# A soft mixture of slots, taken two batches at a time, in a four-layer early-fusion network

## Chip, cores and metric

The kernel runs on one core of a Trainium2 chip as a single program. Its time is the device time of that core in microseconds; the kernel before takes 2536.07 us (median of three runs, 2534.09 to 2538.44). Engine names: PE is TensorE, DVE VectorE, ACT ScalarE, POOL GpSimd, SP SyncE, which issues most DMAs.

## The reference

Sixteen batches, each of 64 image tokens (patches times a matrix) and 128 text tokens, so 192 tokens of width 192. Then four layers, each an attention and a feed-forward part on layer-normalised rows, both added to `h`:

- layer 0: softmax attention, then 8 gated experts, two for each token; layer 1: quantised attention, then 16 experts with GELU, two for each token;
- layer 2: attention with random features, then a tree of 21 nodes; layer 3: softmax attention with 12 heads, then the soft mixture of slots.

The mixture, for x = layernorm(h), 64 experts with 16 slots each (1024 slots):

```
phi_n  = phi * rsqrt(sum over experts of phi^2 + 1e-6)
logits = x . phi_n                       # (batch, 192 tokens, 1024 slots)
D = softmax of logits over the tokens;  C = softmax of logits over the slots
Xs = D^T x                               # 1024 slots of 192 columns
Ys = w2(gelu(w1(layernorm(Xs)) + b1)) + b2   # by expert; hidden width 384
h  = h + C Ys
```

All is float32.

## The kernel before

**Tiles.** `h` lies on 96 partitions: a batch is two tiles of 96 rows by 192 columns, 32 tiles in all, also in the slot stage. `k.xnT` and `phi` have their 192 columns as two halves of 96 rows.

**experts()** (line 480) serves the expert stages of layers 0 and 1. Each of 64 and 56 tiles takes 128 rows. On POOL's queue `fetch(n)` (issue at L539) gathers the rows of tile n into one of three buffers as soon as tile n-3 is turned, and `give(n)` (L545) scatters the answers of tile n when the last product's copy is out. The loop over n issues fetch(n+3), then give(n). PE turns the rows (L564), multiplies them into the hidden columns over 128 rows (L572) and over the other 64 (L578: matmuls of 64 rows, upper and lower half of the array in turn), and down (L584).

**attention3()** (L1543) works in steps of one batch. In a step PE, DVE and ACT take half of the heads at a time, `u`: PE writes logits, DVE takes their lowest (L1860), ACT the exp of the turned ones (L1799), and so on; POOL gives the root of the row variances (L1623), DVE normalises the rows of a coming batch (L1841, L1846). The finished batch is stored to `kept` in device memory and its sums over the rows are taken by take_stats. After the loop `norm_stats` (L150) makes shift and scale of all rows in one block, with a table load on ACT (L186).

**slots_ffn()** (L2372) goes by four quarters of 256 slots (16 experts). `prepare` normalises all rows of `h` on ACT (L2781), turns them, and finds for each token the lowest and highest of its logits over all 1024 slots with rough (bf16) products on PE (L2613) and reduces on DVE (L2874); the result, `low_of`, goes to device memory and comes back by batch as `tok`, spread over 128 partitions, in a ring of three. Then a pass over the 16 batches makes the slots of quarter 0 (`first`), then the quarter's experts run, and in passes 1 to 3 (`both`) the slots of one quarter are made while the answers of the quarter before are weighed and added; `last` weighs those of quarter 3 and writes the output.

In a pass one batch b goes through:
1. PE `make_logits`: 8 matmuls, 96 rows deep, into bank b % 2.
2. DVE `lowest` (L2879) and `shifted` (L2887), which adds `tok` and leaves the combine logits in a ring of HELD = B + 8 batches.
3. ACT `exp_disp` (L2803) with its sum; `exp_combine` (L2808).
4. PE `turn_disp` (bank 4), ACT `keep_disp` (L2820).
5. PE `make_slots` (L2660): 8 matmuls into bank 2 + b % 2.
6. DVE `spread` (sums L2895, aggregates L2901), POOL the root (L2568), DVE `norm` (L2914, L2916).
7. PE `turn_slots` (bank 5), ACT `keep_rows` (L2812).
8. In `both`, LAG = 5 batches behind: PE `weigh` (L2683, 8 matmuls that write 96 rows, bank 6 + b % 2), DVE `add` (L2925). Its answers `ys` come from `s_y` in device memory in FETCHED = 4 buffers.

SP issues, batch by batch and in that order, the tokens (L2469) and the answers (L2476). Every engine's order is written out by hand in its own steps(); nothing plans it. The slot experts' matmuls are L2736 (128 rows), L2742 (64 rows, halves) and L2756.

## Time and profile before

| | |
|---|---|
| median of three runs | 2536.07 us |
| profiled execution, its own time | 2539.78 us |
| its span, from first to last instruction | 2538.0 us |
| mean granted clock of TensorE | 0.956 of full |
| busy: PE, DVE, ACT, POOL | 91%, 52%, 34%, 20% |
| matmuls (L2660, make_slots) | 512, 99.4 us busy, 338 ns each |
| matmuls (L2683, weigh) | 512, 97.3 us busy |
| tokens and answers from memory, share of the last chain | s_tok 2% |

"Busy" counts the time in which an engine executes; matmuls are pipelined and overlap, so that PE's busy share tells only that it hardly stood idle. The mean of one matmul counts its latency and is longer than the distance between two in a stream. The last chain is followed back from the last instruction. Idle time is put down to what ended it.

### The profile page before, as it was taken

The page shows a single profiled execution, that of the slowest core. Times are in us where ns is not written, and L with a number is a line of the kernel's source. Part 1 is how long each engine was busy: PE and PEld are TensorE (multiplying, and loading weights), DVE is VectorE, ACT ScalarE, POOL GpSimd, SP SyncE. Part 2 cuts the span into 40 slices and gives each one's busy share as a digit, 9 for nine tenths or more (in the row PEclk, how much of TensorE's full clock was granted, in tenths as well). Part 3 has the DMA queues.
Part 4 walks back from the last instruction along what each step waited for, and adds up shares of the span by engine and source line. Part 5 has one row for each costly group of instructions (what it writes and reads, how often), then busy time and mean ns, then how long its engine had stood idle before and what let it go on. Part 6 is the DMA issues. An engine that isn't in the chain of part 4 may idle for free. (4 is left out here: it accounts for less than half of the span.)

```text
span 2538.0 us, 52883 instructions
## 1 busy us (share of the span) xinstructions
PE 2315.0 (91%) x18339; PEld 2043.3 (81%) x18339; DVE 1318.6 (52%) x3939; ACT 870.4 (34%) x2148; POOL 514.7 (20%) x621
## 2 busy tenths in 40 slices
PE   9968999997993899998999899999788999999997
PEld 9957999996882789897888787777557888888886
DVE  2664333335996311113888746655576274462744
ACT  2411222223882233332333324433344242432430
POOL 1223233222341444442222100000121010010100
PEclk9979999998995899999999899999899999999999
DMA  4124555521111777672000000000002724527265
GB/s 117 30 53 133 157 149 172 159 77 43 48 30 35 198 235 205 204 216 62 20 20 6 1 14 8 7 7 7 15 16 74 196 71 120 151 57 200 73 159 158
DMA packets 234546, 235.04 MB, mean 93 GB/s; under 512 B 29736, under 2 KB 214942, under 8 KB 234270
## 3 DMA queue, kind: packets, MB, share of 16 engines
q1 hardware_dynamic: 220638, 203.56, 29.0%
q0 software_dynamic: 11520, 27.54, 3.4%
q10 hardware_dynamic: 2240, 1.99, 0.3%
q8 instruction: 90, 1.47, 0.2%
q14 instruction: 58, 0.48, 0.1%
HBM read 277.77 MB, written 35.45 MB: 123 GB/s over the span
## 5 line engine op out<-in xcount | busy, mean ns | idle before, releaser
L572 PE MATMUL f_pg<-f_vxT,f_w 128*128 128x128 f32 x2112 | 260.7, 278 | 3.1 <-DVE f_vxT L642 3.1
L572 PEld LDWEIGHTS f_pg<-f_vxT,f_w 128*128 128x128 f32 x2112 | 256.1, 195 | 4.6 <-DVE f_vxT L642 4.6
L584 PE MATMUL f_po<-f_wd,f_hid 128*128 128x192 f32 x1440 | 254.3, 326 | 1.2 <-DVE f_vout L668 0.6
L584 PEld LDWEIGHTS f_po<-f_wd,f_hid 128*128 128x128 f32 x1440 | 231.2, 190 | 2.0 <-issue 1.7
L545 POOL DMA_INDIRECT f_answers<-f_vout,f_to_row x120 | 118.8, 990 | 423.0 <-DVE f_vout L666 250.4
L653 DVE TENSOR_TENSOR f_hid<-f_silu,f_pg 128x128 f32<-128x128 f32 x336 | 81.8, 284 | 207.1 <-ACT f_silu L621 191.9
L621 ACT ACTIVATE f_silu<-f_pg 128x128 f32<-128x128 f32 x336 | 78.5, 277 | 292.6 <-PE f_pg L578 272.8
L626 ACT ACTIVATE f_hid<-f_pg,f_b 128x128 f32<-128x128 f32 x384 | 106.3, 376 | 196.8 <-PE f_pg L578 196.8
L578 PE MATMUL f_pg<-f_vxT,f_wr 64*128 64x128 f32 x2112 | 151.2, 285 | 0.0
L2568 POOL TENSOR_TENSOR s_small<-s_small,s_half 128x2 f32<-128x2 f32 x64 | 44.5, 695 | 511.3 <-DVE s_small L2904 511.3
L2974 DVE TENSOR_TENSOR s_y<-s_bank,s_b 128x384 f32<-128x384 f32 x64 | 35.5, 558 | 205.2 <-PE s_bank L2756 172.7
L2756 PE MATMUL s_bank<-s_w,s_arena 128*128 128x192 f32 x768 | 135.0, 333 | 7.6 <-DMA s_b<-s_b_of 7.6
L2756 PEld LDWEIGHTS s_bank<-s_w,s_arena 128*128 128x128 f32 x768 | 125.6, 192 | 18.0 <-issue 9.3
L578 PEld LDWEIGHTS f_pg<-f_vxT,f_wr 64*128 64x128 f32 x2112 | 128.1, 188 | 14.7 <-issue 0.6
L642 DVE COPY f_vxT<-f_pt 128x256 f32<-128x256 f32 x120 | 50.6, 422 | 161.2 <-PE f_pt L564 161.2
L2851 ACT ACTIVATE s_arena<-s_bank,s_b 128x256 f32<-128x256 f32 x192 | 73.6, 482 | 165.8 <-PE s_bank L2742 165.8
L539 POOL DMA_INDIRECT f_vrows<-f_normed,f_from_row x120 | 117.0, 975 | 43.2 <-issue 35.6
L2660 PE MATMUL s_bank<-h,s_arena 96*128 96x192 f32 x512 | 99.4, 338 | 21.9 <-ACT s_arena L2820 21.2
L2683 PE MATMUL s_bank<-s_ys,s_combine 128*96 128x193 f32 x512 | 97.3, 339 | 15.7 <-DMA s_ys<-s_y 9.7
L2803 ACT ACTIVATE s_arena<-s_bank,s_small 128x192 f32<-128x192 f32 x128 | 52.7, 417 | 171.9 <-DVE s_combine L2887 171.9
L2660 PEld LDWEIGHTS s_bank<-h,s_arena 96*128 96x128 f32 x512 | 83.7, 192 | 33.9 <-ACT s_arena L2820 33.6
L1860 DVE TENSOR_REDUCE a_low<-a_s_bank 96x6 f32<-96x1152 f32 x64 | 86.7, 1354 | 36.9 <-PE a_s_bank L1642 36.5
(414 smaller groups left out, 4825.8 us busy)
## 6 DMA issues: line engine op xcount, KB each, us to landing
f_wd<-in_L_ffn_W SPq DMA_DIRECT2D x64, 576.0 KB
f_wd<-in_L_ffn_WdT SPq DMA_DIRECT2D x56, 576.0 KB
f_w<-in_L_ffn_W SPq DMA_DIRECT2D x64, 384.0 KB
f_w<-in_L_ffn_WgT SPq DMA_DIRECT2D x56, 384.0 KB
f_w<-in_L_ffn_WuT SPq DMA_DIRECT2D x56, 384.0 KB
s_w<-in_w SPq DMA_DIRECT2D x64, 288.0 KB, 3.8
f_wr<-in_L_ffn_W SPq DMA_DIRECT2D x128, 96.0 KB
s_w<-in_w SPq DMA_DIRECT2D x64, 192.0 KB, 4.2
```

What stands on the lines that cost most here:

```text
L539: pool.indirect_dma_start(out=rows[n % 3][:], out_offset=None, in_=normed, in_offset=bass.IndirectOffsetOnAxis(ap=from_row[:, n:n + 1], ax ...
L545: pool.indirect_dma_start(out=answers, out_offset=bass.IndirectOffsetOnAxis(ap=to_row[:, n:n + 1], axis=0), in_=out[n % 3][:], in_offset=N ...
L572: pe.matmul(pg[j][:, a * ROWS:(a + 1) * ROWS], lift[a][r][:, j * 128:j * 128 + 128], xT[r][:, 0, :], start=(a == 0), stop=False, skip_grou ...
L578: last = pe.matmul(pg[i + s * HALF][:, a * ROWS:(a + 1) * ROWS], rest[a][r][of, i * 128:i * 128 + 128], xT[r][of, 1, :], start=False, stop ...
L584: last = pe.matmul(po[:, 0:D], hid[r][:, j, :], wd[r][:, j, :], start=(at == 0), stop=(at == FC - 1))
L621: nc.scalar.activation(silu[at % 2][:], pg[j][:, 0:ROWS], ACT.Silu).then_inc(gates, 1)
L626: nc.scalar.activation(hid[r][:, j, :], pg[j][:, 0:ROWS], ACT.Gelu, bias=bias[:, ds(e, 1), j:j + 1].rearrange("p o n -> p (o n)")).then_in ...
L653: nc.vector.tensor_tensor(hid[r][:, j, :], silu[at % 2][:], pg[j][:, ROWS:2 * ROWS], ALU.mult).then_inc(hidden, 1)
L1860: nc.vector.tensor_reduce(low[:, :, EACH * c:EACH * c + EACH, DH].rearrange("p t e -> p e t"), s_bank[0:H2, :, 0:2 * N].rearrange("p e (t ...
L2660: last = pe.matmul(split(2 + b % 2, D)[:, c, :], disp[b % 2][:, t, c * 128:c * 128 + 128], h[:, 2 * b + t, :], start=(t == 0), stop=(t == 1))
L2683: last = pe.matmul(split(6 + b % 2, XA, H2)[:, t, :], weights_of(g)[:, c, t * H2:t * H2 + H2], ys[g % FETCHED][:, c, :], start=(c == 0), s ...
L2756: last = pe.matmul(split(6 + s, D)[:, f, :], hid[2 * p + s][:, c, f * 128:f * 128 + 128], w2[2 * p + s][:, c, :], start=(c == 0), stop=(c ...
```

## The change

Three edits.

1. `experts()`: in the loop on POOL give(n-1) follows fetch(n+3), where give(n) did; one more round at the end.
2. `attention3()`: SP brings every finished pair of batches back from `kept` into a new tile `k.x` in another layout: the first 128 tokens of each batch as a full tile, the last 64 of both batches of a pair together as one of 128 rows (three loads a pair). DVE takes the sums of these three (`stats_of_pair`), POOL the root, ACT normalises in place, all between the steps of the attention. The block `norm_stats` before `slots_ffn` goes, and with it the rows' normalisation in `prepare`. `k.phi` is laid out on 128 rows: columns 0 to 127, and columns 128 to 191 twice, once in each half.
3. `slots_ffn()`: passes go by pairs of batches (PAIR = 8), p being a pair and s the batch in it. Products take 128 rows or columns where there were two times 96; what is left of 64 goes through half of the array, the two batches in different halves (`of_half(s)`). Logits take banks 0 and 1, slots 2 and 3, dispT 4, normed rows 5, answers 6 and 7, each for the whole pair. The normalisation of the odd batch's slots moves from DVE to ACT (`norm`, with a bias `nshift` that POOL makes behind the root). The answers are added to a tile `cent` of 193 columns in the same layout (128 rows of each batch, then the 64 left of both), whose last column collects the sum of the weights. HELD = B + 12, LAG = 3 pairs, and SP's order of tokens and answers is by pairs. The slot experts between the passes stay.

```diff
+def bring_pair(sp, k, kept, j, arrived):
+    by_batch = kept.rearrange("(b t) p d -> b (t p) d", t=2)
+    sp.dma_start(k.x[:, 2 * j:2 * j + 2, :], by_batch[2 * j:2 * j + 2, 0:128].rearrange("b p d -> p b d")).then_inc(arrived, 16)
+    for s in range(2):
+        sp.dma_start(k.x[64 * s:64 * s + 64, B + j, :], by_batch[2 * j + s, 128:N]).then_inc(arrived, 16)
...
-            for n in range(NT):
+            for n in range(NT + 1):
                 if n + 3 < NT:
                     fetch(n + 3)
-                give(n)
+                if n:
+                    give(n - 1)
...
+                if b % 2 and b < B - 1:
+                    sp.wait_ge(S["h_kept"], 16 * (b + 1))
+                    if b > 1:
+                        sp.wait_ge(S["x_in"], 48 * (b // 2))
+                    bring_pair(sp, k, kept, b // 2, S["x_in"])
...
+                if m >= 6 and m % 2 == 0:
+                    root_of_pair((m - 6) // 2)
+            root_of_pair(PAIR - 3)
...
+                if pair is not None and u == 1:
+                    act.wait_ge(S["x_shift"], pair + 1)
+                    for at, rows_of in enumerate(thirds_of(pair)):
+                        last = nc.scalar.activation(rows_of, rows_of, ACT.Identity, scale=x_root[:, at, :], bias=x_shift[:, at, :])
+                    last.then_inc(S["x_unit"], 1)
...
+            def stats_of_pair(j):
+                dve.wait_ge(S["x_in"], j * 48 + 48)
+                nc.vector.memset(wide[:, 0:1], 0.0)
+                dve.wait_ge(S["x_unit"], j + 1)
+                nc.vector.memset(wide[:, 1:2], 0.0)
+                for at, rows_of in enumerate(thirds_of(j)):
+                    last = nc.vector.bn_stats(x_sums[:, at, :], rows_of)
+                last.then_inc(S["x_bn"], 1)
+                dve.wait_ge(S["x_bn"], j + 1)
+                nc.vector.memset(wide[:, 2:3], 0.0)
+                for at in range(3):
+                    last = nc.vector.bn_aggr(x_mv[:, at, :], x_sums[:, at, :])
+                last.then_inc(S["x_mv"], 1)
+                dve.wait_ge(S["x_mv"], j + 1)
+                nc.vector.tensor_scalar(x_var[:], x_mv[:, :, 1:2], EPS, None, ALU.add).then_inc(S["x_var"], 1)
...
+                for j in range(2):
+                    answers(o + j)
...
+                for j in range(3, PAIR):
+                    tokens(n + j)
+                for j in range(2, PAIR):
+                    answers(o + j)
...
+            def make_logits(p):
+                q, j = divmod(p, PAIR)
+                if j:
+                    pe.wait_ge(S["dispT"], 2 * p)
+                    pe.wait_ge(S["c_shifted"], 2 * p)
                 for c in range(QC):
-                    for d in range(2):
-                        last = pe.matmul(split(b % 2, N)[:, c, :], phi[:, d, n // B * QS + c * 128:n // B * QS + c * 128 + 128], xnT[:, d, b * N:(b + 1) * N],
-                                         start=(d == 0), stop=(d == 1))
-                last.then_inc(S["logits"], 1)
-            def turn_disp(n, b):
-                pe.wait_ge(S["dispT"], n + b + 1)
-                for t in range(2):
-                    for c in range(QC):
-                        last = pe.transpose(bank[0:H2, 4, t * QS + c * 128:t * QS + c * 128 + 128],
-                                            dispT[b % 2][:, c, t * H2:t * H2 + H2], k.ident[:])
+                    of = slice(q * QS + c * 128, q * QS + c * 128 + 128)
+                    for s in range(2):
+                        pe.matmul(split(s, N)[:, c, :], phi[:, 0, of], xnT[:, j, s * N:s * N + N], start=True, stop=False)
+                    for s in range(2):
+                        last = pe.matmul(split(s, N)[:, c, :], phi[of_half(s), 1, of], xnT[of_half(s), j, 2 * N:3 * N],
+                                         start=False, stop=True)
+                last.then_inc(S["logits"], 2)
+            def turn_disp(p, s):
+                pe.wait_ge(S["dispT"], 2 * p + 2)
+                if s or p:
+                    pe.wait_ge(S["disp"], 2 * p + s)
+                for c in range(QC):
+                    pe.transpose(bank[:, 4, c * 128:c * 128 + 128], dispT[s][:, c, 0:128], k.ident[:])
+                for c in range(QC):
+                    last = pe.matmul(bank[of_half(s), 4, QS + c * 128:QS + c * 128 + 128], dispT[s][:, c, 128:N], k.ident[:], start=True, stop=True)
                 last.then_inc(S["disp_turned"], 1)
-            def make_slots(n, b):
-                pe.wait_ge(S["disp"], n + b + 1)
+            def make_slots(p):
+                j = p % PAIR
+                pe.wait_ge(S["disp"], 2 * p + 2)
+                if p:
+                    pe.wait_ge(S["normed"], p)
+                    pe.wait_ge(S["normed_by_act"], p)
                 for c in range(QC):
-                    for t in range(2):
-                        last = pe.matmul(split(2 + b % 2, D)[:, c, :], disp[b % 2][:, t, c * 128:c * 128 + 128],
-                                         h[:, 2 * b + t, :], start=(t == 0), stop=(t == 1))
-                last.then_inc(S["slots"], 1)
-            def turn_slots(n, b):
-                pe.wait_ge(S["normed"], n + b + 1)
-                if b:
-                    pe.wait_ge(S["rowsT"], n + b)
+                    for s in range(2):
+                        pe.matmul(split(2 + s, D)[:, c, :], disp[:, s * QS + c * 128:s * QS + c * 128 + 128], x[:, 2 * j + s, :],
+                                  start=True, stop=False)
+                    for s in range(2):
+                        last = pe.matmul(split(2 + s, D)[:, c, :], disp[of_half(s), 2 * QS + c * 128:2 * QS + c * 128 + 128],
+                                         x[of_half(s), B + j, :], start=False, stop=True)
+                last.then_inc(S["slots"], 2)
...
+            def weigh(p, at):
+                pe.wait_ge(S["combined"], p + 1)
+                for g in (2 * p, 2 * p + 1):
+                    pe.wait_ge(ys_in[g % FETCHED], (g // FETCHED + 1) * 16)
+                for s in range(2):
+                    g = 2 * p + s
                     for c in range(QC):
-                        last = pe.matmul(split(6 + b % 2, XA, H2)[:, t, :], weights_of(g)[:, c, t * H2:t * H2 + H2],
-                                         ys[g % FETCHED][:, c, :], start=(c == 0), stop=(c == QC - 1))
-                last.then_inc(S["summed"], 1)
+                        pe.matmul(split(at, XA)[:, s, :], weights_of(g)[:, c, 0:128], ys[g % FETCHED][:, c, :],
+                                  start=(c == 0), stop=(c == QC - 1))
+                for c in range(QC):
+                    for s in range(2):
+                        g = 2 * p + s
+                        last = pe.matmul(bank[of_half(s), at + 1, 0:XA], weights_of(g)[:, c, 128:N], ys[g % FETCHED][:, c, :],
+                                         start=(c == 0), stop=(c == QC - 1), skip_group_check=True)
+                last.then_inc(S["summed"], 2)
...
+            def steps(n, o):
+                make_logits(n)
+                for j in range(PAIR + 2):
+                    if j < PAIR:
+                        turn_disp(n + j, 0)
+                        if j + 1 < PAIR:
+                            make_logits(n + j + 1)
+                        turn_disp(n + j, 1)
+                    if j == PAIR + 1 and o is not None:
+                        weigh_in_turn(o + j - LAG)
+                    if j >= 2:
+                        turn_slots(2 * (n + j - 2))
+                    if LAG <= j <= PAIR and o is not None:
+                        weigh_in_turn(o + j - LAG)
+                    if j < PAIR:
+                        make_slots(n + j)
+                    if j >= 2:
+                        turn_slots(2 * (n + j - 2) + 1)
+                if o is not None:
+                    weigh_in_turn(o + PAIR - 1)
...
+            def norm(p):
+                g, u = 2 * p + 1, p % 4
+                act.wait_ge(S["nshift"], p + 1)
+                if p % PAIR >= 2:
+                    act.wait_ge(S["normed_turned"], g - 3)
+                for c in range(QC):
+                    at = QC + c
+                    got = split(3, D)[:, c, :]
+                    nc.scalar.activation(normed[g % 4][:, c, 0:128], got[:, 0:128], ACT.Identity,
+                                         scale=rstd[u][:, at:at + 1], bias=nshift[u][:, at:at + 1])
+                    last = nc.scalar.activation(normed[g % 4][:, c, 128:256].rearrange("p (s n) -> p s n", s=2),
+                                                got[:, 128:D].unsqueeze(1).broadcast_to([128, 2, D - 128]), ACT.Identity,
+                                                scale=rstd[u][:, at:at + 1], bias=nshift[u][:, at:at + 1])
+                last.then_inc(S["normed_by_act"], 1)
...
+            def steps(n):
+                exp_disp(n)
+                exp_combine(n)
+                for j in range(PAIR + 2):
+                    if j < PAIR:
+                        keep_disp(n + j, 0)
+                        keep_disp(n + j, 1)
+                    if j >= 2:
+                        keep_rows(2 * (n + j - 2))
+                    if 1 <= j <= PAIR:
+                        norm(n + j - 1)
+                    if j + 1 < PAIR:
+                        exp_disp(n + j + 1)
+                    if j >= 2:
+                        keep_rows(2 * (n + j - 2) + 1)
+                    if j + 1 < PAIR:
+                        exp_combine(n + j + 1)
...
+            def steps(n, o):
+                lowest(n)
+                shifted(n)
+                for j in range(PAIR + 1):
+                    if j >= 1:
+                        spread(n + j - 1)
+                    if j + 1 < PAIR:
+                        lowest(n + j + 1)
+                        shifted(n + j + 1)
+                    if j >= 1:
+                        norm(n + j - 1)
+                    if j >= LAG and o is not None:
+                        add(o + j - LAG, 6)
+                if o is not None:
+                    add(o + PAIR - 2, 6)
```

## Rows read from the trace of the kernel before

**Rows 1.** Windows, slot passes 0, 1, 3: length, busy (count) PE PEld DVE ACT POOL, clock, DMA

```profile
1880.00:1951.40 71.40, 59.42 (x368) 53.78 (x368) 51.90 (x190) 35.91 (x111) 11.14 (x16) 0.98 0.24 62
...
2026.30:2117.50 91.20, 82.73 (x512) 77.85 (x511) 64.24 (x226) 38.74 (x114) 11.10 (x16) 0.96 0.25 67
...
2343.70:2432.30 88.60, 79.91 (x513) 75.00 (x512) 64.05 (x226) 38.67 (x114) 11.11 (x16) 1.00 0.37 90
```

**Rows 2.** Timeline, second expert stage (start, us, engine, line): turns of tiles 2, 3, 4, 63

```profile
857.08 0.20 PEld L564 LDWEIGHTS f_pt<-ident,f_vrows 128*128 128x128 f32 x2
...
861.61 0.20 PEld L564 LDWEIGHTS f_pt<-ident,f_vrows 128*128 128x128 f32 x2
...
861.59 0.98 POOL L539 DMA_INDIRECT f_vrows<-f_normed,f_from_row  x1 [0.30 <-issue]
...
867.86 0.20 PEld L564 LDWEIGHTS f_pt<-ident,f_vrows 128*128 128x128 f32 x2 [1.84 <-DMA f_vrows<-f_normed,f_from_row]
...
1149.62 0.20 PEld L564 LDWEIGHTS f_pt<-ident,f_vrows 128*128 128x128 f32 x2
```

**Rows 3.** Timeline at a boundary of last attention's steps; groups of lines L2781, L2803

```profile
1641.72 0.17 DVE L1841 TENSOR_SCALAR a_var<-a_mv 96x2 f32<-96x2 f32 x1
...
1642.83 0.66 DVE L1846 TENSOR_SCALAR a_rows<-h,a_mv,a_root 96x192 f32 x2 [0.94 <-POOL a_root L1623]
...
1643.08 1.13 ACT L1799 ACTIVATE a_probT<-a_t_bank 96x1152 f32<-96x1152 f32 x1 [0.20 <-PE a_t_bank L1642]
...
L2781 ACT ACTIVATE h<-h,s_shift,rstd 96x192 f32<-96x192 f32 x32 | 15.5, 535 | 1.0 <-DVE s_shift L2868 1.0
...
L2803 ACT ACTIVATE s_arena<-s_bank,s_small 128x192 f32<-128x192 f32 x128 | 52.7, 417 | 171.9 <-DVE s_combine L2887 171.9
```

**Rows 4.** Timeline from the statistics block to the first slot pass

```profile
1823.30 1.28 ACT L186 ACT_TABLE_LOAD   x1 [13.25 <-PEq L67]
...
1825.72 0.33 SPq L2561 DMA_DIRECT2D s_b_in<-in_b  x1
...
1834.91 38.95 DVE L2874 TENSOR_REDUCE s_low<-s_bank 96x1 f32<-96x1024 f32 x32 [7.70 <-PE s_bank L2613]
```

**Rows 5.** Timeline of VectorE over one batch of slot pass 0

```profile
1893.03 0.55 DVE L2879 TENSOR_REDUCE s_small<-s_bank 128x2 f32<-128x384 f32 x1
...
1893.96 0.62 DVE L2895 BATCH_NORM_STATS2 s_stats<-s_bank 128x6 f32<-128x192 f32 x2
...
1894.69 0.24 DVE L2901 BATCH_NORM_AGGREGATE s_mv<-s_stats 128x2 f32<-128x6 f32 x2
...
1895.94 0.41 DVE L2914 TENSOR_SCALAR s_arena<-s_bank,s_mv,s_small 128x128 f32<-128x128 f32 x1 [0.81 <-POOL s_small L2568]
...
1897.22 0.55 DVE L2879 TENSOR_REDUCE s_small<-s_bank 128x2 f32<-128x384 f32 x1
```

**Rows 6.** Timeline of TensorE, full and half-array matmuls in turn, two stages

```profile
303.56 2.84 PE L572 MATMUL f_pg<-f_vxT,f_w 128*128 128x128 f32 x24
...
306.33 1.61 PE L578 MATMUL f_pg<-f_vxT,f_wr 64*128 64x128 f32 x24
...
307.87 0.44 PE L564 MATMUL f_pt<-ident,f_vrows 128*128 128x128 f32 x2
...
308.15 2.12 PE L584 MATMUL f_po<-f_wd,f_hid 128*128 128x192 f32 x12
...
310.10 2.84 PE L572 MATMUL f_pg<-f_vxT,f_w 128*128 128x128 f32 x24
...
2130.06 2.75 PE L2736 MATMUL s_bank<-s_rowsT,s_w 128*128 128x256 f32 x12
...
2132.74 1.57 PE L2742 MATMUL s_bank<-s_rowsT,s_wr 64*128 64x256 f32 x12
...
2134.24 4.17 PE L2756 MATMUL s_bank<-s_w,s_arena 128*128 128x192 f32 x24
```

**Rows 7.** Windows, a stretch near the second attention's end

```profile
775.00:780.00 5.00, 3.25 (x17) 2.32 (x17) 1.99 (x8) 1.47 (x3) 1.25 (x2) 0.50 0.00 0
```

More of the change, by code:

```diff
@@ L1666, in weigh, with step @@
                 last.then_inc(S["out"], 1)
-            def step(n, u, front, back, late, ahead):
+            def step(n, u, front, back, late, ahead, pair):
                 w = 1 - u
@@ L1793, in keep_raw, with step @@
                 nc.scalar.activation(group(raw, g), o_bank[:, 0:N], ACT.Copy).then_inc(S["raw"], 1)
-            def step(n, u, front, back, late, ahead):
+            def step(n, u, front, back, late, ahead, pair):
                 for c in range(ROUNDS):
@@ L1848, in norm_rows, with step @@
                 last.then_inc(S["rows"], 1)
-            def step(n, u, front, back, late, ahead):
+            def step(n, u, front, back, late, ahead, pair):
                 w = 1 - u
@@ L2414, in slots_ffn @@
-        shift = one("shift", [H2, TILES])
-        low, low_rows = one("low", [H2, TILES]), one("low_rows", [TILES, H2])
+        dispT = [arena[:, u * 2 * N:(u + 1) * 2 * N].rearrange("p (c n) -> p c n", c=QC) for u in range(2)]
+        disp = arena[:, 768:768 + 3 * QS]
+        free = PAIR * PT
+        normed = [part.rearrange("p (c n) -> p c n", c=QC) for part in
+                  (spare[:, free:free + 512], spare[:, free + 512:free + 1024], spare[:, free + 1024:free + 1536], arena[:, 1536:2048])]
@@ L2577, in both @@
             def both(q):
-                for b in range(B):
-                    root(b, (q + 1) * B + b)
+                for j in range(PAIR):
+                    root((q + 1) * PAIR + j)
             def last(q):
```

672 lines of the change are left out of this document (326 added, 346 removed).

## The prediction

> **What bounds the kernel now.** I read the 40 slices first: TensorE (PE) is busy nearly everywhere, so a gain has to come from fewer PE instructions, from a wait of PE that goes, or from a stretch whose limit is another engine. The windows view then gives the limit of each stretch that the change touches. In slot pass 0 no engine is full: of 71.40 us PE has 59.42, VectorE (DVE) 51.90, ScalarE (ACT) 35.91. In passes 1 and 3 PE has 82.73 of 91.20 and 79.91 of 88.60 us [rows 1], so there PE is the bound. The timeline of pass 0 tells what sets its rhythm: DVE goes from one batch's first reduce to the next in 1897.22 - 1893.03 = 4.19 us, and of these it waits 0.81 for GpSimd's root [rows 5]; two batches cost 8.4 us. In passes 1 to 3 two batches cost 90 / 8 = 11.2 us, the ends spread over them. In the second expert stage PE turns one tile's rows every 4.53 us (857.08 to 861.61) where nothing is late, and waits for the gather where it is late [rows 2].
>
> **Experts' rows asked for ahead of answers.** A gather issued at 861.59 is used by the turn at 867.86, which waited 1.84 us for it [rows 2]. From tile 2's turn to tile 63's there are 61 intervals: 1149.62 - 857.08 = 292.5 us against 61 x 4.53 = 276.3. The excess is 16.2 us. After the change fetch(n+3) stands behind give(n-2) on POOL and no longer behind give(n-1): one tile, 4.5 us, earlier, where the late one lacked 1.84. Its own wait (`turned`) has long been met, and the answers go out when they did, since they wait for `outed`. Bounds: -16.2, and 0 if the memory queue itself is what makes gathers late. I take **-16.2**. The first expert stage shows no such wait: 0.
>
> **Rows normalised in the last attention's loop.** At every second step boundary ACT now runs three activations of 128x192 between a_q and the next probT. One of 96x192 took 0.535 us (L2781 in [rows 3]); back to back I take 0.45 each, 1.35 in all. probT starts at 1643.08, 0.20 us after ACT came free, and PE's next round waits for it: nothing covers 1.3 us. The shift that they need is ready, because its root was made a step earlier. At the other boundary DVE runs three bn_stats, three aggregates and small ones behind L1841 at 1641.72: some 1.6 us, to 1643.5, where the next rows start at 1642.83 now [rows 3]. Of these 0.7 us a part delays PE's turn and the first reduce: 0.4. Six pairs: 6 x (1.35 + 0.4) = 10.5. The statistics of each batch move to a place where DVE idles: 0. The three loads a pair, and their wait for the store, have a whole step on SP: 0. In the tail DVE is on the path and gets about 0.4 more. **+10.9**; bounds +3 (ACT finds slack) and +16 (instructions addressed by registers cost more).
>
> **The statistics block goes.** From 1823.30 to 1825.72 [rows 4]: **-2.4**.
>
> **Preparation of phi and of the lows.** Its start takes 1834.91 - 1825.72 = 9.2 us to DVE's first reduce [rows 4]. Now nothing makes rows of unit variance there and fewer fillings run. What is left I estimate at 4.9: the first turn at the low clock 2.0, two copies 0.9, a cast 0.8, four matmuls 1.1. So -4.3. Its body: 32 reduces took 38.95, or 1.22 each [rows 4]; the 24 of the new layout take 29.2 if DVE stays the bound. PE has per pair 16 bf16 matmuls of 512 columns, one group of them on half arrays that can overlap, 2.6 to 3.4; turns 0.8; four changes of array shape (below) 1.5: 5.2 against DVE's 3.65. So PE bounds: 8 x 5.2 = 41.6, +2.6. Sum **-2** (bounds -14, +6).
>
> **Slot passes in pairs: PE's stream.** 12 matmuls of 192 columns took 310.10 - 308.15 = 1.95 us, 0.85 ns a column [rows 6]: 0.16 for 192 columns, 0.11 for 128. Of the three products with 192 columns (logits, slots, weighing) each took 16 matmuls a pair, 2.6 us; now each takes 4 full ones and four halves that run two beside each other, 0.97. The turns of dispT and of the normed rows stay at 8 of 128 columns a pair, 0.9 each. That is 4.7 where 9.6 stood in passes 1 to 3, and 3.7 where 7 stood in pass 0.
>
> But full and half shapes now alternate in groups of two. What that costs stands in two places [rows 6]. In the first expert stage 24 full matmuls of 128 take 306.33 - 303.56 = 2.77 where the stream needs 2.60, and the 24 half ones 307.87 - 306.33 = 1.54 where 12 slots of 0.108 need 1.30: 0.41 for going there and back. In the slot experts, by the same reckoning with 256 columns, 2.68 for 2.60 and 1.50 for 1.30: 0.28. I take 0.38 an excursion, near the upper, because groups of two leave no long matmul beside which the next weights load. Bounds 0 and 0.8 (nothing overlaps). Excursions per pair: logits 2, turning dispT 2, slots 2, weighing 1.
> The Trainium skill, TensorEngine Tiling (Array Packing), section Key Properties, says that a change of tiling mode drains the engine, while a change of tile does not. The trace agrees with its 0.28 to 0.41 us; without that rule the period below would be the 6.5 of the first rival.
>
> **The loop that sets the period.** Banks 0 and 1 (logits), 2 and 3 (slots) now serve a whole pair and are single, so this chain closes on itself: make_logits(p+1), lowest and shifted, norm(p-1) on DVE, make_slots(p), turn_slots, turn_disp(p+1), make_logits(p+2). Lowest plus shifted take 0.93 for one batch (1893.03 to 1893.96); with twice the elements 1.73. Norm takes 1.28 (1895.94 to 1897.22) [rows 5] and 0.13 to its end: 1.41. PE has in it logits 0.97, slots 0.97, turns 0.5 and 0.43, an end of 0.25 that is seen, and four hand-overs of 0.05, together 3.3. That is 6.5. Five excursions lie in the chain: 5 x 0.38 = 1.9. Period **8.4 us**. Beside it: DVE's sums and aggregates took 0.62 and 0.24 and with the small ones 1.17 (1893.96 to 1895.13, where the wait of 0.81 begins) [rows 5], some 2.0 for two batches, so DVE has 1.73 + 1.41 + 2.0 and 0.7 for the add, 5.8; ACT had 35.91 us for 16 batches [rows 1], 4.5 a pair, and gets one batch's norm, about 1.0; PE 4.7 + 2.7 = 7.4. The root is covered by lowest and shifted. Tokens come three pairs ahead and answers two, over 8 us early, so SP's new order costs nothing; were a transfer late, it would cost some 3 us a pair.
>
> Pass 0: a pair cost 8.4 and costs 8.4; the last pair drains two batches at once. **+2.3**.
> Passes 1 to 3: an entry of 4.8 (logits 1.3, lowest and shifted 1.75, four exps at 0.417 [rows 3] 1.7), 7 x 8.4 = 58.8, and an exit of 15.4 (the last slots behind their chain 6.7, spread 2.0, root and product 1.6, norm 1.1, two turns with their copies 2.4, affine 1.6): 79.0 against 91.2, 89.7 and 88.6, of which [rows 1] has the outer two; mean 89.8. **3 x -10.9 = -32.7**.
> The slot experts' loops are untouched: 0. Last loop: two adds, two reciprocals and three products a pair in place of two rounds of such work, but answers still come in four buffers: **-2** (bounds -6, +3).
>
> **Sum.** -16.2 + 10.9 - 2.4 - 2 + 2.3 - 32.7 - 2 = **-42.1 us**. The profiled execution took 2539.8 us (span 2538.0 and 1.8 around it), 3.7 above the median of 2536.1. So 2539.8 - 42.1 = 2497.7, or 2494 on the scale of the median.
>
> **Rivals.** The period's price moves with the price e of an excursion: 5 x 7 x 4 = 140 in the passes, 32 in preparation, 172 us per us of e.
> (A) Changes of shape are nearly hidden: e = 0, period 6.5, 0.38 x 172 = 65 less, 2429. For it: in the slot experts the way in costs 0.08. Against: the way out costs 0.20 and 0.24 [rows 6].
> (B) Changes of shape cost more in short groups; place, PE in the passes and the preparation. The sum turns at e = 0.38 + 42 / 172 = 0.62 and is +30 at 0.8: 2566, slower than before. For it: with two matmuls a group the weight load, the matmul and its end may all lie bare, 0.11 + 0.16 + 0.1 each way. Against: 0.41 is the highest that the rows show.
> (C) The clock falls in pass 0. There PE would have 3.7 + 2.3 of 8.4 us. A stretch with PE 3.25 of 5.00 us busy ran at 0.50 of the full clock [rows 7], 1.2 and not 2.4 GHz; pass 0 had 83% and 0.98 [rows 1]. PE's 3.7 doubles, of which the loop feels 2 a pair, 8 x 2 = +16: 2510.
> The Trainium skill, TensorE: Matmul & The Clock Gate, section What's actually happening, calls the low clock the default that activity lifts; the trace agrees.
> (D) Gathers stay late, because the expert weights' traffic makes them so: the 16.2 stays, 2510. For it: this gather took 6.3 us from issue to use, with nothing but transfers before it. Against: it would have been wanted 4.4 us after its issue, and is wanted 8.9 after it now.
>
> **Chances.** Forecast 0.55, (A) 0.19, (B) 0.07, (C) 0.10, (D) 0.09. A measurement of this kernel tells a change of 0.2% (5 us) from none. (B) is slower but for its lower end: slower 0.06, same 0.04, faster 0.90. The range 2432 to 2525 leaves out (B) and the end of (A) and of the sum's bounds, about 2 in 10; within the forecast alone it is 2475 to 2515.
>
> **What would show it.** Right: no DMA waits at L564 in the second expert stage, and turns every 4.53 us; in the last attention, boundaries that are 1.3 and 0.4 us longer in turn; the statistics block gone; pairs in the passes 8.4 us apart by the exp of dispT, with gaps in PE's weight loads at each change from full to half; passes 1 to 3 79 us long. Wrong: a period of 6.5 or over 9, waits for tokens or answers in the passes, a clock under 0.9 in pass 0, a second expert stage as long as before.

## The result, and the profile after

The changed kernel takes 2622.51 us (median of four runs, 2616.14 to 2631.96) against 2537.26 before (2534.09 to 2545.39 in four): a ratio of 1.033, 95% interval 1.030 to 1.036. It is slower by 85 us where 42 less were forecast, and outside the range. Its profiled execution took 2627.83 us, its span is 2626.1, 88.1 above the span of before.

The page of the changed kernel: span, the busy times of the engines, the slices of the granted clock, and one group by line.

```profile
span 2626.1 us, 52947 instructions
...
PE 2379.2 (91%) x18479; PEld 2004.8 (76%) x18479; DVE 1238.4 (47%) x3647; ACT 899.9 (34%) x2232; POOL 511.2 (19%) x621
...
PEclk9979999999986999989998988998888999899999
...
L2739 PE MATMUL s_bank<-x,s_arena 128*128 128x192 f32 x256 | 69.3, 402 | 32.3 <-ACT s_arena L2923 13.0
```

From the last attention on, seven of the 17 slices of the granted clock show an 8, where one did before; the mean is 0.932 against 0.956. The group is the key to the largest error: `make_slots` has 4 full-array products in the code for a pair, 128 in all, and the trace has 256 matmuls. A float32 product is two matmul instructions.

Stage by stage, the boundaries read from the first instruction of each stage in both timelines (us):

| stretch | before | after | forecast of the change | measured |
|---|---|---|---|---|
| up to tile 2 of the second expert stage | 857.1 | 855.7 | 0 | -1.4 |
| second expert stage, tiles 2 to 63 | 292.5 | 276.6 | -16.2 | -15.9 |
| then to the last attention's first reduce | 332.0 | 337.9 | 0 | +5.9 |
| its first to its last reduce | 308.6 | 335.2 | +10.9 with the tail | +26.6 |
| tail, statistics block, preparation | 83.8 | 83.4 | -4.4 | -0.4 |
| slot pass 0 | 79.5 | 115.7 | +2.3 | +36.2 |
| three expert parts between passes | 208.7 | 204.5 | 0 | -4.2 |
| passes 1 to 3 | 270.1 | 307.4 | -32.7 | +37.3 |
| last experts and last loop | 105.7 | 109.6 | -2 | +3.9 |

The second expert stage is as it was forecast. Timeline of the changed kernel, turns of tiles 2, 3 and 63 (start, us, engine, line):

```profile
855.68 0.21 PEld L530 LDWEIGHTS f_pt<-ident,f_vrows 128*128 128x128 f32 x2
...
860.22 0.20 PEld L530 LDWEIGHTS f_pt<-ident,f_vrows 128*128 128x128 f32 x2
...
1132.28 0.20 PEld L530 LDWEIGHTS f_pt<-ident,f_vrows 128*128 128x128 f32 x2
```

4.54 us from one turn to the next and (1132.28 - 855.68) / 61 = 4.53 over all of them; the waits of [rows 2] are gone.

The slot passes are not. Windows of the changed kernel, passes 0, 1 and 3 (columns as in [rows 1]):

```profile
1888.80:2004.50 115.70, 87.65 (x418) 58.55 (x417) 41.30 (x141) 48.51 (x139) 9.64 (x16) 0.78 0.15 43
...
2074.34:2175.07 100.73, 88.54 (x545) 61.84 (x545) 47.43 (x156) 48.36 (x138) 9.64 (x16) 0.97 0.22 64
...
2413.06:2516.47 103.41, 91.22 (x546) 63.35 (x545) 47.81 (x156) 48.35 (x138) 9.64 (x16) 0.93 0.25 74
```

In pass 1 DVE's busy time fell by a quarter (64.24 to 47.43), but PE's went up from 82.73 to 88.54, where the forecast had 8 x 7.4 = 59. In pass 0 the granted clock is 0.78; it was 0.98. ("Lowest" is VectorE's reduce over a pair's logits; the time from one to the next is the period of a pair below.)

### The profile page after: what moved, and what is told of

Its sections match the earlier page's. It is cut to its first block and busy times, and to the rows that moved or that the text cites. A ratio compares the mean times of both kernels' runs of the same rounds, so it can differ in the third digit from the quotient of the medians.

```text
span 2626.1 us, 52947 instructions
## 1 busy us (share of the span) xinstructions
PE 2379.2 (91%) x18479; PEld 2004.8 (76%) x18479; DVE 1238.4 (47%) x3647; ACT 899.9 (34%) x2232; POOL 511.2 (19%) x621
## 3 DMA queue, kind: packets, MB, share of 16 engines
q1 hardware_dynamic: 219750, 206.18, 27.6%
## 5 line engine op out<-in xcount | busy, mean ns | idle before, releaser
L2604 POOL TENSOR_TENSOR s_small<-s_small,s_half 128x4 f32<-128x4 f32 x32 | 32.2, 1006 | 585.1 <-DVE s_small L3033 585.1
L3096 DVE TENSOR_TENSOR s_y<-s_bank,s_b 128x384 f32<-128x384 f32 x64 | 35.5, 557 | 201.7 <-PE s_bank L2840 172.8
L2963 ACT ACTIVATE s_arena<-s_bank,s_b 128x256 f32<-128x256 f32 x192 | 73.5, 481 | 165.5 <-PE s_bank L2826 165.5
L2739 PE MATMUL s_bank<-x,s_arena 128*128 128x192 f32 x256 | 69.3, 402 | 32.3 <-ACT s_arena L2923 13.0
L2820 PE MATMUL s_bank<-s_rowsT,s_w 128*128 128x256 f32 x384 | 91.0, 388 | 2.2 <-issue 2.2
L1787 ACT ACTIVATE a_probT<-a_t_bank 96x1152 f32<-96x1152 f32 x64 | 72.0, 1125 | 43.3 <-PE a_t_bank L1630 43.1
L1630 PE MATMUL a_t_bank<-a_q_low,a_k 32*96 32x192 f32 x768 | 70.2, 372 | 17.0 <-ACT a_probT L1787 16.8
```

The source lines that it names most:

```text
L2739: pe.matmul(split(2 + s, D)[:, c, :], disp[:, s * QS + c * 128:s * QS + c * 128 + 128], x[:, 2 * j + s, :], start=True, stop=False)
L2820: pe.matmul(bank[:, HC3 * s + c, 0:256], w1[2 * p + s][:, c * 128:c * 128 + 128], rowsT[:, 0, 2 * i + s].rearrange("c b p -> c (b p)"), st ...
```

## Where it went, as the trace tells

**One pair of a full-speed pass.** Timeline of the changed kernel, PE from a pair's logits (L2715 full-array, L2717 half-array) over the turns of dispT (L2726, L2728), the turns of the normed rows (L2754), a weighing (L2765, L2770) and the slots (L2739 on), to the next turns:

```profile
2123.83 0.92 PE L2715 MATMUL s_bank<-h,phi 128*128 128x192 f32 x4
...
2124.68 0.60 PE L2717 MATMUL s_bank<-h,phi 64*128 64x192 f32 x4
...
2125.21 0.92 PE L2715 MATMUL s_bank<-h,phi 128*128 128x192 f32 x4
...
2126.05 0.60 PE L2717 MATMUL s_bank<-h,phi 64*128 64x192 f32 x4
...
2126.58 0.44 PE L2726 MATMUL s_bank<-ident,s_arena 128*128 128x128 f32 x2
...
2127.53 0.66 PE L2754 MATMUL s_bank<-ident,h 128*128 128x128 f32 x4
...
2128.02 1.48 PE L2765 MATMUL s_bank<-s_ys,s_combine 128*128 128x193 f32 x8
...
2129.43 0.88 PE L2770 MATMUL s_bank<-s_ys,s_combine 128*64 128x193 f32 x8
...
2130.36 0.89 PE L2739 MATMUL s_bank<-x,s_arena 128*128 128x192 f32 x4
...
2133.08 0.66 PE L2754 MATMUL s_bank<-ident,h 128*128 128x128 f32 x4
...
2133.57 0.38 PE L2726 MATMUL s_bank<-ident,s_arena 128*128 128x128 f32 x2
```

Logits run 4 full (two products), 4 half, 4 full, 4 half: 0.85, 0.53, 0.84 and 0.53 us, together 2126.58 - 2123.83 = 2.75. Their stream is 8 x 0.1625 for the full ones and 4 x 0.1625 for the eight half ones, which run two beside each other, 1.95 in all, and 0.8 for two excursions (from full-array to half-array matmuls and back) remains. The forecast had 0.97 and 0.76.

The next pair's logits start at 2134.46. So PE's 10.63 us for a pair are logits 2.75, slots 2.72, weighing 2.34, turns of dispT 0.95 and 0.89, turns of the normed rows 0.49 twice. By the prediction's sizes these are 1.73, 1.73, 1.35, 1.66 and 0.9, together 7.4. The windows view of the changed kernel over one such pair shows that nothing else is in it:

```profile
2116.07:2126.70 10.63, 10.58 (x69) 7.51 (x70) 5.77 (x20) 5.79 (x17) 1.20 (x2) 1.00 0.19 58
```

PE is busy for 10.58 of the 10.63 us, at full clock, and waits for no other engine. In the kernel before, two batches at the end of pass 3 took 10.06 us (eight batches from 2371.09 to 2411.32): each product with 192 columns 2.6, and the turns of dispT, eight single instructions, 0.9 where there are now four single ones and eight half-array ones.

**A boundary of the attention.** Timeline of the changed kernel, ACT and PE:

```profile
1601.17 0.65 ACT L1774 ACTIVATE a_q<-a_s_bank 128x576 f32<-128x576 f32 x1 [2.48 <-PE a_s_bank L1621]
...
1601.72 1.41 ACT L1800 ACTIVATE x<-x,a_x_shift,a_x_root  x3
...
1603.04 1.11 ACT L1787 ACTIVATE a_probT<-a_t_bank 96x1152 f32<-96x1152 f32 x1
...
1604.20 0.90 PE L1630 MATMUL a_t_bank<-a_q_low,a_k 32*96 32x192 f32 x12 [0.86 <-ACT a_probT L1787]
...
1606.33 1.60 PE L1630 MATMUL a_t_bank<-a_q_low,a_k 32*96 32x192 f32 x12 [0.58 <-ACT a_probT L1787]
```

a_q, then the three normalisations in 1.41, then probT; PE waits 0.86 for it and 0.58 at the next round. At 1606.33 the same 12 matmuls take 1.60 instead of 0.90. The windows view shows that this is the clock: the whole attention, the step before, and a stretch right after those waits:

```profile
1470.16:1805.40 335.24, 321.60 (x3199) 252.10 (x3200) 178.56 (x366) 124.32 (x193) 15.08 (x20) 0.92 0.04 12
...
1582.81:1602.92 20.11, 19.68 (x211) 15.54 (x212) 11.42 (x24) 8.04 (x15) 1.15 (x2) 1.00 0.09 24
...
1608.00:1612.00 4.00, 4.00 (x40) 2.64 (x38) 1.67 (x2) 1.45 (x2) 0.00 (x0) 0.50 0.00 0
```

0.50 of the full clock is 1.2 and not 2.4 GHz. Of the five steps that begin so before the last reduce, two (from 1602.92 and 1650.27) fell in this way and took 27.2 and 25.7 us for 20.0; the others took 1.0 more than before. From the last reduce to the first instruction of `slots_ffn` it took 39.1 us (1805.4 to 1844.5) where it had taken 35.5 (1790.2 to 1825.7) with the statistics block still in it: there the normalisation stands behind VectorE's 3.6 us reduce over phi, and PE waited 5.8 us. The preparation behind it took 44.3 for 48.3, 4 less where 2 less were forecast.

**Pass 0.** Timeline of the changed kernel, PE around one `make_slots`:

```profile
1939.18 0.89 PE L2739 MATMUL s_bank<-x,s_arena 128*128 128x192 f32 x4 [2.17 <-ACT h L2923]
...
1940.52 1.49 PE L2739 MATMUL s_bank<-x,s_arena 128*128 128x192 f32 x4
...
1941.94 1.01 PE L2742 MATMUL s_bank<-x,s_arena 64*128 64x192 f32 x4
...
1942.89 1.11 PE L2754 MATMUL s_bank<-ident,s_arena 128*128 128x128 f32 x4
```

PE waits 2.17 for ACT's normalisation of the odd batch, here and in the other steady pairs, and after it the clock falls: the first 4 + 4 matmuls take 1.34 us, the same again 1942.89 - 1940.52 = 2.37. A pair costs 12.2, later 13.6 us, in passes 1 to 3 10.63.

**The end of a pass.** Timeline of the changed kernel, the full-array part of each weighing behind the last `lowest` of pass 3 (2489.35):

```profile
2490.68 1.48 PE L2765 MATMUL s_bank<-s_ys,s_combine 128*128 128x193 f32 x8
...
2499.59 1.48 PE L2765 MATMUL s_bank<-s_ys,s_combine 128*128 128x193 f32 x8
...
2506.54 1.48 PE L2765 MATMUL s_bank<-s_ys,s_combine 128*128 128x193 f32 x8
...
2509.95 1.58 PE L2765 MATMUL s_bank<-s_ys,s_combine 128*128 128x193 f32 x8 [0.54 <-DVE s_cent L3055]
...
2514.16 1.48 PE L2765 MATMUL s_bank<-s_ys,s_combine 128*128 128x193 f32 x8
```

Five weighings stand behind the last batch's logits, four of them in what I had called the exit; at 2.3 us each they are 9 us that the sum left out. From the last `lowest` to the experts' first product the three passes take 27.1 us each; in the kernel before they took 21.9, 21.9 and 21.0, so that of the 37 us by which passes 1 to 3 grew 17 stand at their ends.

## The experiments

The kernel before ran beside each on the same chip; its medians there were 2543.18 us (the first four below) and 2536.40 (the others). Ratios are to it, and 1.0333 is the changed kernel's; a difference between two kernels is the difference of their ratios times 2537 us.

**The experts' reordering alone** (on the kernel before).

```diff
-            for n in range(NT):
+            for n in range(NT + 1):
                 if n + 3 < NT:
                     fetch(n + 3)
-                give(n)
+                if n:
+                    give(n - 1)
```

> The kernel before with the experts' reordering alone: fetch(n+3), then give(n-1). Of the changed kernel's trace the second expert stage took 276.6 us from tile 2's turn to tile 63's where it took 292.5 before. Theory: this edit is independent of the others and is worth those 16 us: 0.6% faster than before, about 2520 us, with no wait for gathered rows. Rival: gathers come in time in the changed kernel by chance of the memory's traffic, and alone the edit gives less than 5 us.

Measured: 2529.42 us, ratio 0.995 (0.993 to 0.997), 13 us less (7 to 19 by the interval), which leaves out the rival. The edit stands by itself. Its trace also showed that the last attention's steps 1 and 2 (the first one is step 0) take 27.2 and 25.8 us in a kernel without the rest of the change, so 10 of the 26.6 us belong neither to the attention's edit nor to the slots'; the profiled execution of before had 22.9 and 20.0 there. Windows of this kernel, steps 1 and 2:

```profile
1488.40:1541.40 53.00, 51.16 (x409) 39.07 (x410) 20.53 (x40) 15.88 (x25) 1.37 (x2) 0.71 0.01 4
```

**The normalisation inside the step** (on the changed kernel; VectorE's shift moves with it, ahead of `q_low`).

```diff
+                if pair is not None and u == 1:
+                    act.wait_ge(S["x_shift"], pair + 1)
+                    for at, rows_of in enumerate(thirds_of(pair)): ...
                 if back:
                     keep_raw(n - 1, GROUPS - 1, not late)
                 if ahead:
                     keep_qkv(n + 1, 1 - u, ...)
-                if pair is not None and u == 1: ...
```

> The changed kernel with ScalarE's three normalisations moved inside the step, ahead of the copy of the last raw group, where ScalarE waited 7.8 us for TensorE; x_shift on VectorE ahead of q_low. All else is the same. Theory: the third attention lost 26.6 us (308.6 to 335.2 between its first and last reduce) because the 1.4 us of ScalarE ahead of the next exp leave TensorE idle at a boundary, and in four steps its clock then fell to 0.50 for some 13 us; with the work covered, all steps take 20.0 to 20.2 us and the attention 310 us, so 25 us less than the changed kernel. Rival: the loads of x and VectorE's statistics are what disturbs the steps (the clock falls in even steps as well); then the steps of 26 to 27 us stay and the gain is under 8 us.

Measured: 2606.06 us, ratio 1.0247 (1.022 to 1.028), 22 less than the changed kernel. The steps from 3 on take 20.0 to 20.1 us, the last 18.8 as before. Windows of this kernel, from the attention's second reduce to its last:

```profile
1465.50:1784.50 319.00, 310.87 (x3173) 244.05 (x3174) 176.79 (x365) 125.30 (x192) 15.09 (x20) 0.95 0.05 12
```

The first reduce stands at 1463.02, so first to last take 321.5 us against 335.2: 14 and not 25, since the clock fell in steps 1 and 2 here too (27.7 and 26.9; 27.1 and 25.9 in the changed kernel); another 5 came from the tail. Pass 0, which has no edit here, took 4 us more (120.1). The loads and VectorE's statistics, still in their place, cost 0.1 us a step. The theory holds; for the stretch it named, its size was 11 us too large, because it took the start for the edit's.

**Idle products in pass 0** (on the changed kernel).

```diff
                     if j < PAIR:
+                        if o is None:
+                            fill(pe, k, bank[:, 7], 8)
                         make_slots(n + j)
```

> The changed kernel with eight idle products of the identity (into a bank that pass 0 does not use) ahead of make_slots in slot pass 0, where TensorE waits 2.2 us for ScalarE. They compute nothing that is used. Theory: pass 0 takes 115.7 us at a granted clock of 0.78 because that wait lets the clock fall in each pair; with it filled the clock stays at 1.0, the period of a pair goes from 12.2 (later 13.6) to 10.6, as in passes 1 to 3, and the pass to about 97: 18 us less. Rival: the pass is long for its chain alone, and 1.7 us of added TensorE work a pair leave it as it is or lengthen it by up to 14 us.

Measured: 2604.25 us, ratio 1.0238 (1.021 to 1.027), 24 less. Windows of this kernel, pass 0:

```profile
1885.11:1987.78 102.67, 86.11 (x546) 62.95 (x545) 41.25 (x141) 48.63 (x139) 9.64 (x16) 0.94 0.17 49
```

102.7 us for 115.7, the steady period 10.6 for 12.2 to 13.6, the clock 0.94 for 0.78. More work on PE made the pass shorter. The 97 expected left out that its first pair and its end ran slow as well. The pass gives 13 of the 24 us; where the rest comes from was not found (the two ratios' intervals allow 13 to 35).

**Full ahead of half** (on the changed kernel). In this form the second column group opens its sum in a bank where the first one's is half made, so that the first group's full-array part is lost; number, size and order of the matmuls are what is timed.

```diff
                 for c in range(QC):
-                    of = slice(q * QS + c * 128, q * QS + c * 128 + 128)
                     for s in range(2):
-                        pe.matmul(split(s, N)[:, c, :], phi[:, 0, of], xnT[:, j, s * N:s * N + N], start=True, stop=False)
+                        pe.matmul(split(s, N)[:, c, :], phi[:, 0, of[c]], xnT[:, j, s * N:s * N + N], start=True, stop=False,
+                                  skip_group_check=True)
+                for c in range(QC):
                     for s in range(2):
-                        last = pe.matmul(split(s, N)[:, c, :], phi[of_half(s), 1, of], xnT[of_half(s), j, 2 * N:3 * N],
-                                         start=False, stop=True)
+                        last = pe.matmul(split(s, N)[:, c, :], phi[of_half(s), 1, of[c]], xnT[of_half(s), j, 2 * N:3 * N],
+                                         start=False, stop=True, skip_group_check=True)
...
```

> The changed kernel with the products of logits and of slots in another order: all full-array matmuls of both column groups, then all half-array ones, so one change of shape and back for each product in place of two. Same matmuls in number and size. Theory: a pair's logits take 8 full and 8 half matmuls in the trace (each product is two instructions), 1.95 us of stream, and two excursions at 0.4: 2.74 measured; grouped they take 2.35, the slots likewise, and a pair costs 0.8 less: 32 pairs, 25 us less in all, a little more where the clock stays up. Rival: half-array matmuls simply do not overlap fully and a change costs nothing; then grouping changes nothing (within 3 us).

Measured: 2578.71 us, ratio 1.013 (1.009 to 1.017), 51 less. Timeline of this kernel, one pair's logits:

```profile
2109.53 1.57 PE L2715 MATMUL s_bank<-h,phi 128*128 128x192 f32 x8
...
2111.03 0.92 PE L2719 MATMUL s_bank<-h,phi 64*128 64x192 f32 x8
...
2111.88 0.44 PE L2728 MATMUL s_bank<-ident,s_arena 128*128 128x128 f32 x2
```

2111.88 - 2109.53 = 2.35, as expected, and the steady periods are 9.84 for 10.63, 0.8 less. So an excursion costs 0.39 us. Grouping also puts more matmuls between the two that add to one sum; that this is not what costs is seen in the weighing, whose full and half parts are different sums: 2.34 for a stream of 1.95, again 0.39 for its one excursion. The run gave twice the 25 expected: in its trace passes 1 to 3 take 283 us for 307.4 (the 24 of the reckoning, with their ends), pass 0 takes 99.8 for 115.7, as three of its seven periods are over 10 us in place of six, and the attention 6 less, where one step fell in place of two. That the clock falls less often with shorter waits is what these two suggest, not what was tested.

**The three together** (in the grouping only the first product of a bank opens the sum).

> The changed kernel with all three mendings together: normalisation inside the attention's step, idle products in slot pass 0, full-array products of logits and slots grouped ahead of the half-array ones (here only the first product of a bank opens its sum, so both column groups keep their partial sums). Theory: the three causes are separate and their gains add: a period of 9.8 us in every pass, no fall of the clock after the attention's first steps, passes 1 to 3 of 95 us each, pass 0 of 90: 16 + 18 + 44 less than the changed kernel, 2545 us, the same as before within 0.5%. Since the experts' reordering is in it and worth some 14, pairs and the rest are then still 14 us worse than what they replaced. Rival: the mendings overlap and it stays over 2565.

Measured: 2565.10 us, ratio 1.010 (1.008 to 1.012), 59 less than the changed kernel and not 78: at the rival's line. Windows of this kernel, passes 0 and 3:

```profile
1870.96:1968.08 97.12, 80.24 (x545) 64.26 (x545) 41.27 (x141) 48.71 (x139) 9.65 (x16) 0.91 0.19 52
...
2362.53:2457.98 95.45, 83.24 (x547) 64.05 (x545) 47.42 (x156) 48.44 (x138) 9.66 (x16) 0.95 0.27 78
```

Passes 1 to 3 are the 95 us expected. Pass 0 has 97 for 90. The mendings overlap: pass 0 is 13.0 us shorter with the idle products, 15.9 with the grouping and 18.6 with both, and the attention 13.7 shorter with its normalisation inside, 6.2 in the trace of the grouping and 13.7 here. Steps 1 and 2 of the attention still take 27.6 and 27.0. With all three the passes still take 97.1 and 286 us where 79.5 and 270.1 stood.

**ScalarE's normalisation first.** `norm(n + j - 1)` ahead of `keep_rows(2 * (n + j - 2))`, and six idle products a pair in pass 0 where the last kernel had eight; otherwise as the last.

> As the combined kernel, with ScalarE's normalisation of the odd batch ahead of the copy of the even batch's turned rows (and six idle products for eight in pass 0). Theory: in passes 1 to 3 TensorE is full by now (no wait over 0.4 us in a period of 9.8), so they stay; in pass 0 the chain over ScalarE's norm sets the period and it goes from 9.8 to 9.3: 4 us less in all. Rival: the chain bounds all passes and each period falls by 0.5: 15 us less.

Measured: 2557.20 us, ratio 1.007 (1.004 to 1.009), 9 less than the last, with intervals that overlap. Periods 9.37 for 9.84 in pass 0, 9.74 in the others. In pass 0 of the last kernel `make_slots` waited 0.39 us for ACT in each steady pair, here it waits 0.4 for VectorE: the loop over ACT's normalisation bounded that pass. In the other passes PE waits for nothing in a steady pair of either kernel (9.78 of 9.84 and 9.74 of 9.74 us busy): there PE itself is the bound.

**Without the halves** (on the changed kernel; logits lose the last 64 columns, slots the last 64 tokens).

> The changed kernel without the half-array matmuls of logits and of slots: of the logits it leaves out the last 64 columns, of the slots the last 64 tokens. Theory: the halves and their two changes of shape cost 1.4 us of each product's 2.74 a pair, more than the 0.65 that they stream; without them each product takes 1.30, and the period of passes 1 to 3 falls from 10.6 to 7.8, some 85 us in all. Rival: by the prediction's own sizes a product's halves were worth 0.33 and two excursions 0.76 a pair, 1.1 for each product, and the period falls by 2.2 to 8.4, some 68 us in all.

Measured: 2526.30 us, ratio 0.993 (0.990 to 0.997), 101 less. Timeline of this kernel, VectorE's `lowest` in pass 1, then PE:

```profile
2080.58 0.96 DVE L3000 TENSOR_REDUCE s_small<-s_bank 128x4 f32<-128x768 f32 x1 [0.82 <-PE s_bank L2715]
...
2088.42 0.96 DVE L3000 TENSOR_REDUCE s_small<-s_bank 128x4 f32<-128x768 f32 x1 [0.82 <-PE s_bank L2715]
```

```profile
2084.11 1.54 PE L2736 MATMUL s_bank<-x,s_arena 128*128 128x192 f32 x8
...
2085.49 0.60 PE L2748 MATMUL s_bank<-ident,h 128*128 128x128 f32 x4
...
2086.81 1.57 PE L2715 MATMUL s_bank<-h,phi 128*128 128x192 f32 x8
...
2088.22 0.38 PE L2723 MATMUL s_bank<-ident,s_arena 128*128 128x128 f32 x2
```

The period is 2088.42 - 2080.58 = 7.84: the theory's 7.8 and not 8.4. Slots take 2085.49 - 2084.11 = 1.38, logits 1.41: the halves, a third of each product's work, cost 1.4 us of 2.75. Of the 101 us, where 85 were expected, passes 1 to 3 give 69 in the trace and pass 0 gives 28. At full clock the period is 7.84 there as well, with PE 5.67 us busy and waiting 2.2 for ACT: so the loop alone, without a weighing, is as long as PE's own work with one.

**A better version.** The kernel before with the reordering, and seven idle products in the attention's second step, ahead of the turn of the lows.

```diff
+                if isinstance(n, int) and n == 1:
+                    pe.wait_ge(S["xT"], n + 2)
+                    fill(pe, k, turns, 7)
                 if front:
                     pe.wait_ge(S["low"], n * ROUNDS + ROUNDS)
```

> The kernel before with the experts' reordering and seven idle products of the identity in the second step of the last attention, where TensorE waits 1.5 us for VectorE and the clock then fell for 13 us in most traces (steps 1 and 2 of 27.2 and 25.8 us; 22.9 and 20.0 in the trace of before). Theory: a short wait is what lets the clock fall; with it filled steps 1 and 2 take some 21 and 20 us, so 10 us less than the reordering alone, about 2517 on the scale where that took 2529. Rival: the clock falls there for the attention's low activity as a whole; then the steps stay at 27 and 26 and the seven products cost 1 us.

Measured: 2518.37 us, ratio 0.992 (0.990 to 0.994), faster than both kernels. Windows of this kernel, the same two steps as in the reordering alone:

```profile
1487.50:1527.10 39.60, 38.85 (x424) 30.50 (x424) 20.47 (x41) 15.82 (x25) 1.37 (x2) 1.00 0.02 5
```

39.6 us for 53.0, clock 1.00 for 0.71: 19.6 and 20.0 us for 27.2 and 25.8. The expected 10 is 13 in the trace and 8 by the ratios, whose intervals overlap. The two traces speak for the theory, but each is of one execution, and the one of before had 22.9 and 20.0 with no idle products; what the times show is that the kernel with both edits is faster than before.

## Why the prediction was wrong

The steps of the prediction, with what the runs showed:

- **Experts' rows.** Right: -16.2 forecast, -15.9 in the trace, and alone 13 us on the chip. Rival (D) is out.
- **PE's stream in pairs: the step that failed.** "Of the three products with 192 columns each took 16 matmuls a pair, 2.6 us; now each takes 4 full ones and four halves". The 16 (and the "8 matmuls" of a batch ahead of the prediction) were counted in the profile, where a float32 product is two matmuls; the 4 and 4 were counted in the code. In one unit it is 16 against 8 and 8, and the stream goes from 2.6 to 1.95 and not to 0.97. The price of an excursion, 0.38, was right (0.39 measured), but two of them, 0.8, are now more than the 0.65 saved: as it is written, with full and half in turn, the product takes 2.75 us where the old one took 2.6. The counts were there to read in the row of L2644 or L2660, x512 for 64 batches at four calls each.
- **The loop's period.** 8.4 was forecast, 10.63 measured, and the miscount is in it twice over. Added to the loop, 0.97 for logits and for slots gives 10.3, and in pass 0 with idle products the period is 10.63; but the loop goes over ScalarE's normalisation of the odd batch, which `make_slots` waited for, and not over VectorE's as it was written down. Added to PE's own 7.4, where the weighing has it as well, it gives 10.3 too, and in passes 1 to 3 this is what bounds: PE is busy for 10.58 of 10.63 us and waits for nothing. That PE would be the bound there was left out because its sum was 3 us short. Seven periods of 10.63 are 15 us over the forecast's 58.8. In the trace they took 70.9, 73.5 and 73.5 us in passes 1 to 3, 41 too much in all, and the longer logits at each entry add 4.
- **A pass's exit.** 15.4 forecast. From the last `lowest` to the experts the forecast has 18.9 and the trace 27.1: the weighings that the lag of three pairs leaves behind were not in the sum. 8 us a pass, 25 in all. With the 41 and the 4 this is the 70 by which the three passes missed their forecast. This is read from the timeline; no run took it away.
- **Pass 0.** Rival (C) had it: the clock falls. It was given 16 us over the forecast. Of the 34 that pass 0 took beyond it, 15 are the period, 13 come back in the trace with idle products, and the rest is a first pair and an end that ran slow in both.
- **Attention.** +1.3 at each boundary was right (1.41 of ACT, 1.0 in a step's length at full clock), and +0.4 for VectorE too high (0.1). What was missed is that PE's waits of 0.9 and 0.6 at the boundary can be followed by a fallen clock: 6 us a time, two times of five, and in none of the steps of the two traces where the waits were taken away. The place for the work was in the trace: ahead of the copy of the last raw group ACT waited 4.6 us for PE in a step at full clock (7.8 in a slow one), and there the same work cost 0.1. Of the +26.6, 16 are the edit's and 10 the start's.
- **Statistics block and preparation.** The block went and the preparation took 4 us less, better than the 2 forecast; the tail, 6 us longer with PE's wait behind the reduce over phi, ate both; 0.4 had been put down for it.
- **Open**: the 5.9 us between the experts and the last attention lie in code that no edit touches. In five traces of kernels that are the same up to there (the changed one, normalisation inside, idle products, grouped, the three together) this stretch took 329.6 to 338.8 us, so that 5.9 is within what differs from one execution to the next. The 5.9 by which the last loop missed its forecast were not followed.
- **Rival (B)** gave the right side by the wrong mechanism: the price of an excursion did not move, the work between the excursions was twice as much.

The Trainium skill, TensorEngine Tiling (Array Packing), section Key Properties, sets a drain against each change of mode and lets tiles work in parallel. The runs fit the first, with 0.39 us an excursion, though the drain itself is in no row; they agree with the second: 8 half-array matmuls of 192 columns took 0.85 us, 0.2 for the change among them, where one after another they would need 1.30.

## What to carry to other kernels

Count before and after in the same unit, and take it from the instruction counts of a row: a float32 product is two matmuls in the profile and one call in the code, a transposition one and one. Splitting a product into full and half parts paid here only with the halves gathered into one group (2.35 us for 2.6); with two excursions at 0.39 us it ate more than the 0.65 saved (2.75). Add up the busiest engine's own period by the instructions of a trace before a chain of waits is taken for the bound. Working by pairs also leaves more work behind the last pair (27.1 us for 21 to 22 at the end of each pass). Work on another engine that makes a full PE wait is to be priced with the slow clock that can follow (here 6 us for waits of 1.4 in all, two times of five), and it is worth looking for the place inside the step where that engine waits anyway.

## What the runs showed of the hardware that I had not expected

- Adding TensorE work shortened two stretches: 8 idle products a pair took pass 0 from 115.7 to 102.7 us, 7 idle products took two attention steps from 53.0 to 39.6.
- The same wait did not always bring the clock down: of five boundaries with the same 0.9 and 0.6 us of waiting, two were followed by a clock of 0.50 for some 13 us and three by none. The same two fell in the trace with idle products in pass 0, only the first of them in the grouped kernel.
